# The carry of a blocked scan by shifted copies and VectorE instead of TensorE, with two small reorderings before it

## The reference

```python
# cross part: embeds = layernorm(x), patch = ctx
h = rmsnorm(embeds, g_res) @ W_in.T + b_in
u = c * rmsnorm(ctx, g_init)[:, :512]          # c = exp(-0.001)
s[t] = A * s[t-1] + u[t]                        # A = 1 - exp(-0.001), about 0.001
bidx = cumsum(mask) - 1
plug = clip(cumsum(boundary_mask(bidx)) - 1, 0, 3201)
x = x + s[plug] + h
# feed-forward part
n = layernorm(x)
x = x + gelu(n @ w1 + b1) @ w2 + b2             # 512 -> 2048 -> 512
```

## Time and profile before

| | us |
|---|---|
| median of 3 runs | 851.11 (848.03 to 851.15) |
| profiled execution, its own time | 851.29 |
| its span | 849.6 |
| PE busy | 836.3 (98%) |
| DVE busy | 317.7 (37%) |
| ACT busy | 286.7 (34%) |
| POOL busy | 254.5 (30%) |
| mean granted TensorE clock | 0.996 |

### The profile page before, as it was taken

The page is one execution under the profiler, slowest core; times in us unless marked ns, Lnnn a source line. Parts: engine busy times, 40 slices in busy tenths (PEclk is TensorE's granted clock), DMA queues, the critical chain, the costliest instruction groups (busy, mean ns, idle before and its releaser), DMA issues.

```text
span 849.6 us, 10756 instructions
## 1 busy us (share of the span) xinstructions
PE 836.3 (98%) x3786; PEld 686.3 (81%) x3786; DVE 317.7 (37%) x511; ACT 286.7 (34%) x522; POOL 254.5 (30%) x236
## 2 busy tenths in 40 slices
PE   7998999999999999999999999999999999999998
PEld 5886888888888888888888887888888888888886
DVE  5899772434342232424151424134113311241112
ACT  4664245542532234222622243222222322222221
POOL 2263265980262016310532043202500250011000
PEclk9998999999999999999999999999999999999999
DMA  9758688160215111231115021402300140010001
GB/s 229 237 146 293 189 220 302 49 166 8 74 51 142 29 62 61 79 92 49 53 69 123 0 74 49 97 0 100 49 1 1 50 94 5 0 50 0 1 1 50
DMA packets 34968, 71.07 MB, mean 84 GB/s; under 512 B 5716, under 2 KB 5716, under 8 KB 33176
## 3 DMA queue, kind: packets, MB, share of 16 engines
q1 hardware_dynamic: 25964, 58.91, 21.2%
q0 software_dynamic: 4608, 8.39, 6.4%
q10 hardware_dynamic: 4368, 3.42, 1.4%
HBM read 47.87 MB, written 22.84 MB: 83 GB/s over the span
## 4 chain that ended last, share of the span: by engine, by line
PE 91%; DVE 6%; issue 1%; ACT 1%; DMA 1%; POOL 1%; ACTq 0%; DVEq 0%; POOLq 0%
PE acc L843 15%; PE acc L845 15%; PE acc L844 15%; PE h_bank L845 14%; PE h_bank L843 14%; PE h_bank L844 14%; PE t_bank L902 2%; DVE h_lo L1025 1%; DVE st_a L1020 1%; DMA g_res_c<-in_L_xattn_g_res_dram 1%; PE acc L838 1%; DVE cl L1039 1%; PE t_bank L831 1%; PE t_bank L875 1%; DVE xa_odd L1033 0%
## 5 line engine op out<-in xcount | busy, mean ns | idle before, releaser
L1242 DVE TENSOR_TENSOR h_lo<-g_f,h_hi 128x512 fp32r<-128x512 f32 x128 | 100.3, 784 | 450.4 <-ACT g_f L780 450.4
L778 ACT ACTIVATE h_hi<-h_bank,b_c 128x512 fp32r<-128x512 f32 x128 | 88.1, 689 | 441.2 <-PE h_bank L845 436.3
L843 PE MATMUL h_bank<-xt_hi,w_hi 128*128 128x512 f32 x512 | 201.9, 394 | 0.0
L843 PE MATMUL acc<-w_hi,h_hi 128*128 128x512 f32 x512 | 199.8, 390 | 0.0
L845 PE MATMUL h_bank<-xt_hi,w_lo 128*128 128x512 f32 x512 | 199.4, 389 | 0.0
L844 PE MATMUL h_bank<-xt_lo,w_hi 128*128 128x512 f32 x512 | 199.3, 389 | 0.0
L845 PE MATMUL acc<-w_hi,h_lo 128*128 128x512 f32 x512 | 199.2, 389 | 0.0
L844 PE MATMUL acc<-w_lo,h_hi 128*128 128x512 f32 x512 | 199.2, 389 | 0.0
L844 PEld LDWEIGHTS h_bank<-xt_lo,w_hi 128*128 128x128 f32 x512 | 96.2, 188 | 21.0 <-issue 1.2
L843 PEld LDWEIGHTS h_bank<-xt_hi,w_hi 128*128 128x128 f32 x512 | 96.1, 188 | 20.8 <-issue 1.2
L845 PEld LDWEIGHTS h_bank<-xt_hi,w_lo 128*128 128x128 f32 x512 | 96.1, 188 | 20.1
(11 more groups left out here) (164 smaller groups left out, 700.7 us busy)
## 6 DMA issues: line engine op xcount, KB each, us to landing
out_dram<-x_cur SPq DMA_DIRECT2D x32, 256.0 KB, 2.1
x_next<-x_part SPq DMA_DIRECT2D x7, 1024.0 KB, 4.8
w_raw<-in_L_ffn_w_dram SPq DMA_DIRECT2D x6, 1024.0 KB, 9.0
scan_table<-cl SPq DMA_DIRECT2D x6, 896.0 KB
ch<-in_ctx_dram SPq DMA_DIRECT2D x20, 256.0 KB, 2.9
cl<-in_ctx_dram SPq DMA_DIRECT2D x5, 1024.0 KB
xa_even<-in_x_dram SPq DMA_DIRECT2D x16, 256.0 KB, 5.2
xa_odd<-in_x_dram SPq DMA_DIRECT2D x16, 256.0 KB, 5.8
```

Of the source, the lines that this page charges most:

```text
L778: act.activation(h_hi[:, m % HB, :], h_bank[m % 2][:], ACT.Gelu, bias=b1_c[:, m:m + 1])
L843: nc.tensor.matmul(dst, a_hi, b_hi, start=first, stop=False)
L1242: dve.tensor_tensor(h_lo[:, m % HB, :], g_f32[:], h_hi[:, m % HB, :].bitcast(F32), ALU.subtract).then_inc(h_split, 1)
```

## The change

It has five parts.

1. In the feed-forward groups the carry is made without TensorE. With t the last rows of all partitions, SP copies t one partition down into ch[:, 0]; VectorE adds A^4 times it to t, giving a sum over two partitions in ch[:, 1]; SP copies this two partitions down; VectorE adds A^8 times it, giving the sum over four; SP copies that one partition down into ch[:, 0], which add_carry reads. The copies move 127, 126 and 127 partitions of 2 KB.
2. In groups 1 to 4 the squares of rows 2 and 3 both stand at m 1, scale_rows at m 3 and the scan at m 4, the adds at m 5 and 6, add_carry at m 7. In group 0 scale_rows stays at m 4, the scan at m 5; the adds stand at m 6 and 7 and add_carry at m 8.
3. `count_before` stands at tile 20, behind the carry of block 1 and two tiles of products, and `finish_plug` at tile 20. `gather_indices(0)` stands before the gathers at tile 22.
4. The first copies: g_res_c is the first of ScalarE's queue, then the first two input tiles; all four parts of W_in are in SP's queue.
5. The warm-up has 14 transposes, not 20.

```diff
-WARM = 20
+WARM = 14
@@ block.sync
-            for k in range(2, K):
+            for k in range(K):
                 sp.dma_start(win_raw[:, k, :], win_v[:, k, :]).then_inc(win_loaded[k], 16)
-            sp.dma_start(xa(0), x_v[0, :, 0, :]).then_inc(xa_loaded[0], 16)
...
+            def shift_sums(g):
+
+                wait_apart(sp, l3_ready, NA + g + 1)
+                sp.dma_start(ch[1:P, 0, :], cl[0:P - 1, R - 1, :]).then_inc(shifted, 16)
+                wait_apart(sp, part_summed, 2 * g + 1)
+                sp.dma_start(ch[2:P, 0, :], ch[0:P - 2, 1, :]).then_inc(shifted, 16)
+                wait_apart(sp, part_summed, 2 * g + 2)
+                sp.dma_start(ch[1:P, 0, :], ch[0:P - 1, 1, :]).then_inc(shifted, 16)
...
-            for t in range(1, 8):
+            for t in range(2, 8):
                 load_tile(t)
...
                 if scan:
+                    shift_sums(g)
                     store_block(b, cl)
@@ block.gpsimd
                 if t == 22:
                     scales(24, TI)
+                    pool.wait_ge(plug_ready, 1)
+                    gather_indices(0)
                     wait_apart(pool, table_stored, STORED + BLOCK_STORED * 2)
...
-                if t == 20:
-                    pool.wait_ge(plug_ready, 1)
-                    gather_indices(0)
@@ block.scalar
-            for k in range(2):
-                act.dma_start(win_raw[:, k, :], win_v[:, k, :]).then_inc(win_loaded[k], 16)
             act.dma_start(g_res_c[:], g_res.rearrange("(k p) -> p k", p=P),
                           allow_slow_non_contiguous=True).then_inc(g_res_loaded, 16)
+            for t in range(2):
+                act.dma_start(xa(t), x_v[0, :, t, :]).then_inc(xa_loaded[t], 16)
...
-                    if scan and not first and m <= 2:
+                    if scan and not first and m < 2:
                         b = NA + g
-                        for j in ((0, 1), (2,), (3,))[m]:
+                        for j in (2 * m, 2 * m + 1):
...
-                    if scan and m == 4:
+                    if scan and m == 3 + first:
                         scale_rows(NA + g, cl, rc, range(R))
@@ block.tensor
                 if t == 18:
-                    count_before()
                     pe.wait_ge(block_ready, 1)
                     carry(1, cl_next, acc[3][:])
+                if t == 20:
+                    count_before()
...
-                    if scan and m == 6:
-                        carry(NA + g, cl, t_bank[0][:])
@@ block.vector
+            def sum_rows(g, i):
+
+                dve.wait_ge(shifted, 16 * (3 * g + i + 1))
+                rows = (cl[:, R - 1, :], ch[:, 1, :])[i]
+                dve.scalar_tensor_tensor(ch[:, 1, :], ch[:, 0, :], A ** (R * (i + 1)), rows, ALU.mult, ALU.add).then_inc(part_summed, 1)
+
             def add_carry(b, carry, rows, js):
-                if 0 in js:
+                if not isinstance(b, int) or b >= NA:
+                    dve.wait_ge(shifted, 16 * (3 * (b - NA) + 3))
+                elif 0 in js:
                     dve.wait_ge(carried, b + 1)
...
-                if t == 19:
+                if t == 20:
                     finish_plug()
...
-                    if scan and m == 5:
+                    if scan and m == 4 + first:
                         for j in range(1, R):
                             scan_row(NA + g, cl, j)
-                    if scan and m == 7:
-                        add_carry(NA + g, t_bank[0][:], cl, range(R))
+                    if scan and m == 5 + first:
+                        sum_rows(g, 0)
+                    if scan and m == 6 + first:
+                        sum_rows(g, 1)
+                    if scan and m == 7 + first:
+                        add_carry(NA + g, ch[:, 0, :], cl, range(R))
```

More of the change, by code:

```diff
@@ L316, in xattn_ffn @@
         carried = sem("carried")
+        shifted = sem("shifted")
+        part_summed = sem("part_summed")
         block_ready = sem("block_ready")
```

## The result

The changed kernel takes **890.29 us** (median of 4 runs, 886.64 to 892.19), the kernel before 850.25 (848.03 to 851.15): a ratio of 1.047, 95% interval 1.0449 to 1.0491. It is slower by 4.7%. The forecast was 872.3 us, its range ended at 890.0. The profiled execution is the lowest of the four, 886.64 us, with a span of 884.9.

The account below looks back on a forecast made before the run. TensorE bounds the kernel, busy 836.3 of 849.6 us. Front -6.9, group 0 +12.6, groups 1 to 3 +11.7 and group 4 +3.5 give +20.9 on 851.29: 872.3 us; eight-in-ten range 852 to 890, leaving out spread copies.

Parts of the forecast that it names:

- The copies: Shifted copies in scan groups: 127 rows on one DMA engine take 12.2 us, the middle 126 rows about 2.2.
- the front: Ahead of the groups: sooner start and shorter wait at tile 18, together -6.9 us, bounds -2.5 and -8.5.
- rival 1: Scan groups: copies spread over all engines land in 2.1 to 3 us, only gains are left, 839.4 us; chance 0.12.
- TensorE waits 3.5 us: Groups 1 to 3: h_lo of m 8 ends at 365.8, wanted at 362.3, so 3.5 us of idle each.
- I count 1.3: Clock cost behind each gap of groups 1 to 3: 1.3 us, bounds 0 and 2.9.
- The idle is just over the 3.3 after which the clock fell: Gaps of groups 1 to 3: 3.5 us of idle against 3.3 at tile 18; a fall costs 2.9 us.
- rival 2: All six gaps: the clock falls in each, 2.9 us instead of 1.3, copies at upper price, 886.5 us; chance 0.25.
- Group 0: First feed-forward group: 11.5 us of delay in all, +2 for the clock, -0.91 for the carry: +12.6 us.
- The gathers: After add_carry: the first gather lands at 376.5, its statistics stand at 378.8; covered by 2 us, so no cost.
- the wait at tile 18: TensorE's wait for the scan rows: about 2.7 us, under the 3.3 after which the clock fell; tile ends 7.3 sooner.
- The five carries: Carries of groups 0 to 4 off TensorE: 4 x 0.91 + 1.31 = 4.95 us less.
- The port: add_carry reading two SBUF operands beside POOL: each row could be 1 us longer, but POOL is idle, nothing charged.

Follow-up runs that it names:

- the split copies: The changed kernel with each shifted copy issued as two, 112 rows and the 14 or 15 left: 841.81 us, ratio 0.9914; run again 841.45 us.
- Filling the gap: The changed kernel with 48 unread transposes on TensorE ahead of the second product of m 8 in groups 1 to 4: 880.23 us, ratio 1.0354.
- the front alone: The kernel before with only the load order, warm-up of 14 and count_before two tiles later: 844.54 us, ratio 0.9938; run again 845.12 us.

## Why the prediction was wrong in size

**Direction and mechanism were right, but for how often the clock falls.** The copies on one engine, VectorE's order, h_lo as the one that TensorE waits for, one gap in each of groups 1 to 4 and two in group 0, the plain groups at 89.12, the front sooner: all of it is in the trace, and the split copies show that the length of the copies makes the loss. The split version even gives rival 1's time, 839.4 forecast and 841.5 to 841.8 measured.

**The step that failed is the price of a gap**, "TensorE waits 3.5 us" and "I count 1.3" for the clock, times four. It was 5.88 us of idle (5.90, 5.94, 5.80, 5.88) and 2.2 of clock (96.72 to 97.74 less 89.12 less the idle: 2.7, 1.7, 2.8, 1.7), 8.1 us a gap where the sum had 4.8. Over four groups that is 13 us, all but 1.3 of the 14.4 by which the place-by-place sum was short (35.3 against 20.9); group 0's 2.9 more and the front's 1.6 less make up the rest. Two causes:

- *The copies.* From the end of the scan rows to the end of h_lo of m 8 the sum said 32.1 us; in group 3 it is 33.84 (445.44 to 479.28). The third copy is 13.0 us from issue in place of 12.2, the middle one 3.1 in place of 2.2, and the first ends 0.4 us later behind the scan rows than said. I had taken 0.085 us a packet and a fixed part of 1.4 us from stores that ran on 16 engines. The busy time of the third copy's packets (11.9 us where I had 10.8) puts the miss into the packets; the line through the four row counts (0.084 a row and 2.3) and the middle copy, which misses as much with nine packets an engine, put it into the fixed part. The times don't separate the two. TensorE also ran dry 0.5 us sooner. 1.7 + 0.5 are nearly all of the 2.3 us by which this gap was missed. A gap is the difference of two sums: an error of 5% in a chain of 32 us and one of 2% in its deadline became two thirds of the gap.
- *The clock.* It fell at **every** one of the six gaps, that of 3.61 us in group 0 too. "The idle is just over the 3.3 after which the clock fell" took one observation for a threshold, and falls came at shorter gaps as well (last section). What a fall costs depends on how much of the low stretch lies behind the gap: the mean clock is 0.63 and 0.60 over the 7.0 and 6.7 us behind the gaps of groups 1 and 3, some 2.6 us lost, and 0.72 and 0.73 over 5.3 and 5.9 us behind those of groups 2 and 4, some 1.5 lost. Filling the gap showed the clock's part by itself. This is rival 2, which had 0.25 where the forecast had 0.40. That its 886.5 is so near the profiled execution's 886.64 is partly luck: it is 0.9 us short on each gap of groups 1 to 4 and has 1.7 too much for group 0 and 1.6 too little gain in the front, and the median is 890.29.

**Group 0**, forecast +12.6, is +15.45. Idle of 3.61 and 6.70 us for h_lo, 10.3 where I had 11.5, 0.6 for w_lo and 0.3 for n_rows, the carry's 0.9 less, and of what is left of the 15.45, 5.2, two falls of the clock are 4.6 (mean clock 0.76 over 7.2 us and 0.63 over 7.7; 2 forecast). The waiting of the first copy behind the x_next load, which this sum had, is there. The gathers were called covered by 2 us in groups 1 to 4. They were, but only because the gap shifted TensorE as well; in group 0 n_rows came 0.3 us late, and with the copies still long and the adds moved out of the way it was late in all five.

**The front**, forecast -6.9, is -8.46 in the changed kernel's trace. The start was right (first product at 5.57, 5.70 forecast), and so was the wait at tile 18 (2.11, forecast 2.7). But the full gain is luck: ten traces of kernels with this or the count_before edit stood still there for 2.1 to 2.3 us, and behind it the clock fell in six and stayed up in four. The changed kernel's own trace is one of the four. By the medians the front gives 5.7 and 4.5 us. The mean clocks of the single executions bear this out: of the 13 of the front alone, 5 have a mean clock of 1.000 and a median of 842.9 us, and 8 have 0.998 and 845.1. It does not explain why the median of the changed kernel (890.3) is 3.6 above its profiled execution: the mean clock is 0.976 in that one and 0.977, 0.977 and 0.975 in the others. That spread stays open.

**The five carries** were worth what was said in groups 1 to 4 (90.03 to 89.12, the last one 90.48 to 89.12, of which 0.4 is the earlier scan's) and nothing in group 0. **The port** was told right: where an add stood beside POOL's work it took 1.1 to 1.8 us against 0.69, and no wait of TensorE came of it. The Trainium skill (SBUF — State Buffer, "SBUF: two separate sides") says that a VectorE operation with two SBUF inputs and a GpSimd operation that reads SBUF take turns at a shared port; the durations agree with it.

## What to carry to other kernels

Before moving data across partitions by DMA, factor the number of rows: if it is prime, or its largest divisor up to 16 is small, cut it into a piece with a multiple of 16 rows and the rest; here that one edit was worth 48 us. When a chain of waits is longer than an engine's slack, price the gap as a difference with the errors of both sums in it, count a fall of the clock in full behind a gap of four microseconds or more (it came every time here) and as a risk behind one of two or three, and ask which later bound the gap will cover. A profiled execution holds one outcome for each short wait of TensorE, so a gain of a few microseconds there is read from medians or from several traces.

## What was not expected of the hardware

- TensorE's clock fell at the waits of 2.1 to 2.3 us at tile 18 in 6 of 10 traces, each time to the lower of its two levels (granted 0.50), in some only after TensorE had been at work again for over a microsecond, as behind the 2.18 us above. The same kernel has both outcomes: the front alone in its two traces, for one. At the first products, near 13 us, it fell behind a wait of 1.98 us in the kernel with only the last copy whole and of 1.87 in the second trace of the split copies, and not behind one of 1.97 in the front's second. Of the 22 waits of 2.57 us or more behind TensorE's first products in all the traces it fell at 21. The one without a fall is a wait of 3.65 us, in group 0 of the kernel with only the groups' half of the change; the 3.61 us at the same place in the changed kernel had one.
- The 1 MB load of x_next holds a copy that runs on one engine, but the copy doesn't always come later for it. Issued 0.44 us behind the load (group 0), it took 15.25 us. Issued 2.5 us behind it (group 3), it took 12.98 against 13.04 for the third copy, though none of its packets of 2 KB had started 2.0 us after issue, as the row below shows (445.5 to 447.5: 15 small packets and nothing else under 8 KB). In the rest of the time (447.5 to 458.3) the engines' share is 6.4% of 16 for 10.8 us, 11.1 us for its packets, where the third copy's took 11.9. Why they were quicker is open.

```profile
DMA packets 100, 0.70 MB, mean 348 GB/s; under 512 B 15, under 2 KB 15, under 8 KB 15
```

- So a packet of 2 KB on an engine that works alone took 0.087 us in one copy and 0.093 in the other.
